# A state-space scan on Trainium2: one scan per block with the carried state as its initial value

## The chip, the cores and the metric

The kernel runs on one core of a Trainium2 chip. The metric is the device time of one execution in microseconds (us). The engines that the text names are TensorE (PE, and PEld for its weight loads), VectorE (DVE), ScalarE (ACT), GpSimd (POOL) and SyncE (SP), which issues most of the DMAs. Each engine has an instruction queue of its own that it works through in order, and the queues are tied together by semaphores.

## The reference, cut to what matters

The layer is a macaron: a feed-forward part with ternary weights (d = 512, 2048 hidden), a Mamba-like mixer, and the feed-forward part again, over 4 sequences of 1024 tokens, each part with a layernorm and a residual. The change touches only the recurrence of the mixer:

```
D, E, N = 512, 1024, 16
def step(h, inp):                       # h: (batch, E, N), zero at a sequence's start
    d_l, B_l, C_l, x_l = inp
    A_bar = jnp.exp(d_l[:, :, None] * A)
    h = h * A_bar + (d_l * x_l)[:, :, None] * B_l[:, None, :]
    y_l = jnp.einsum('ben,bn->be', h, C_l)
    return (h, y_l)
```

Channels are E = 1024 (8 blocks of 128 partitions), and each channel has N = 16 states.

## The kernel before

The 4096 tokens are cut into 16 chunks of CH = 256 tokens (4 chunks a sequence). A chunk's recurrence is worked in STEPS = 32 steps: the first 16 for the channel blocks 0 to 3 ("half 0"), one state n each, the last 16 for the blocks 4 to 7 ("half 1"). So a step S = 32 x chunk + s handles one state of four blocks of 256 tokens, 1024 columns on 128 partitions. Four engines share a step, and a ring of four buffers `h[:, s % RING]` goes round between them:

- POOL, `u_times_b` (L725): `h` = u x B, 1024 columns (L743). Then, since the scan starts from zero at each block's head, it waits for its own product (`ub_step`) and adds the first state's contribution to column 0 of the four blocks (L747, four columns). It releases `ub_ready`. Ahead of the product stand waits for the planes of B (`bb_loaded`), for the ring slot (`hT_ready` or `times_c`) and for `carry_saved`.
- ACT, `exps` (L981): the decays exp(delta x A) for the columns 1 to 255 of each block, in PSUM, two activations for each of two tiles `abar[0]` and `abar[1]` of two blocks. Column 0 of each block stays zero (set once, L1407), so that one scan can run through two blocks and starts afresh at the second one. A tile can be refilled once the scan of the step before has read it.
- DVE, `scan_of` (L1287): two `tensor_tensor_scan`s a step, each over 512 columns (two blocks), with the constant 0.0 as initial value (L1294), in place in `h`.
- ACT, `save_carry` (L993): the last column of each block goes to `carry`. PE, `states_T` (L1515): eight transposes of `h` into PSUM (L1522), and DVE, `y_add` (L1303), adds them into y, scaled by C (L1323, the first of a half L1320). For 8 to 10 steps of a chunk ("elem" steps) POOL multiplies by C instead (`state_times_c`, L757) and adds the product into `xw` by a DMA that accumulates (L761).

The first state of a chunk is made once per half: ACT's `first_decay` (L998) computes exp(delta[0] x A) for 16 states of four blocks (L1003, four activations), DVE's `mask_carry` (L1296) zeroes the carry where a sequence begins, POOL's `first_state` (L763) multiplies both (L768) into `a0`, which L747 adds.

The rest of the layer runs beside this, on the same engines: PE's matmuls of the feed-forward part (L1560, L1571), of the projections (L1583, L1593, L1613, L1632), their evacuation by ACT and DVE, the convolution (DVE L1367, L1376), softplus (ACT, POOL L809), u = delta x x (POOL L850), and POOL's low halves of the hidden values (`hidden_low`, L842). The order is written out by hand: the tables FILL_SLOTS, FIRST_SLOTS, LOOP_SLOTS and LAST_SLOTS say for each of 32 slots of a phase which PE jobs stand in it, and each engine's queue follows from them with fixed offsets (exps 2 slots ahead of the step, the product 3 ahead, the scan 1 ahead, and so on). The phases are fill, first, 14 times loop, last, drain. SP reloads a pair of B's planes (`load_planes`, L647) when POOL's products have used the old one, by `ub_ready`.

Of the kernel before, what the change touches and what calls it, by code (L numbers as in the profile page):

```python
# [21 lines left out]
P = 128  # L22
# [4 lines left out]
CH = 256  # L27
# [196 lines left out]
ACTS = 2  # L224
XD_0 = 3
# [88 lines left out]
def elems_before(c, s):  # L314

    whole = [len(elem_of(k)) for k in range(c)]
    return sum(whole) + sum(k < s for k in elem_of(c))

# [95 lines left out]
def macaron_kernel(nc, resid, norm_w, W_skip, W_in, conv_w, conv_b, W_delta_1, W_delta_2, b_delta_2, W_B, W_C,  # L414
# [12 lines left out]
    with ctx:  # L427
# [40 lines left out]
        a0 = sb("a0", [P, 2, HE, N])  # L468
# [54 lines left out]
        abar_zero = sem("abar_zero")  # L523
# [8 lines left out]
        ub_step, ub_ready, abar_ready = sem("ub_step"), sem("ub_ready"), sem("abar_ready")  # L532
        a0_ready, masked, x0_ready = sem("a0_ready"), sem("masked"), sem("x0_ready")
# [49 lines left out]
        def _(sp):  # L583
# [116 lines left out]
        def _(pool):  # L700
# [24 lines left out]
            def u_times_b(i, s):  # L725
# [3 lines left out]
                if s == 0 or q > planes_of(s - 1):  # L729
                    need(pool, bb_loaded[q % 2], 16 * planes_loaded(i, q))  # L730
                if s % N == 0:
                    if S:
                        u_of(i, half, S)
                    need(pool, u_ready, 2 * i + half + 1)
                    need(pool, x0_ready, 2 * i + half + 1)
# [3 lines left out]
                elif S >= RING:  # L739
# [3 lines left out]
                pl.tensor_tensor(h[:, s % RING, :, :], u[:, :, :],  # L743
                                 bb[:, planes_of(s) % 2, s % PLANES:s % PLANES + 1, :].broadcast_to([P, HE, CH]),
                                 ALU.mult).then_inc(ub_step, 1)
                need(pool, ub_step, S + 1)
                pl.tensor_tensor(h[:, s % RING, :, 0], h[:, s % RING, :, 0], a0[:, half, :, n], ALU.add).then_inc(ub_ready, 1)  # L747

            def state_times_c(i, s):
# [7 lines left out]
                pl.tensor_tensor(hc[:, :, :], h[:, s % RING, :, :], cplane[:, k:k + 1, :].broadcast_to([P, HE, CH]),  # L757
# [87 lines left out]
            def u_of(c, half, S):  # L845
                need(pool, ub_ready, S)
# [19 lines left out]
            def run(ph, i):  # L866
# [3 lines left out]
                for s in range(STEPS):  # L870
# [13 lines left out]
                    for q in range(QT):  # L884
                        if after(ph, f"YT_{q}", 0, s):
                            gated(ph, i, q)
                    for kind, p in hidden_units(ph, s):
                        hidden_low(ph, i, kind, p)
# [4 lines left out]
                    if ph != "fill" and after(ph, "D2_1", 3, s):  # L893
                        first_state(i + 1, 0)
                    if after(ph, "D2_3", 2, s):
                        softplus(i, 1)
                    if after(ph, "D2_3", 3, s):
                        first_state(i, 1)
# [10 lines left out]
        def _(sc):  # L909
# [71 lines left out]
            def exps(i, s):  # L981
# [4 lines left out]
                for r in range(2):  # L986
                    need(sc, scanned, 2 * S - 1 + r)
                    for e in range(2):
                        k = half * HE + 2 * r + e
                        ins = ac.activation(abar[r][:, e, 1:], delta[:, k, 1:], ACT.Exp, scale=a_neg[:, k, n:n + 1])  # L990
                    ins.then_inc(abar_ready, 1)

            def save_carry(i, s):  # L993

                need(sc, scanned, 2 * (STEPS * i + s + 1))
                ac.activation(carry[:, s // N, :, state_of(s)], h[:, s % RING, :, CH - 1], ACT.Copy).then_inc(carry_saved, 1)
# [730 lines left out]
```

## Time and profile before

| | |
|---|---|
| median of 3 runs (lowest to highest) | 2941.11 us (2938.22 to 2942.51) |
| the profiled execution | 2940.29 us, its span 2938.7 us |
| busy over the span | PE 90%, DVE 86%, POOL 82%, ACT 65% |
| mean granted clock of TensorE | 0.97 of full speed |
| one loop iteration (from 1026.40 to 1197.32 us) | 170.92 us |

The profile is one execution. Its page gives busy shares by engine, the chain of work that ended last (followed back from the last instruction to what released it), the costliest groups of instructions and the idle time in front of them. A busy time is a union, so where an instruction starts a little before its predecessor on the same engine has ended, count x mean is more than busy. The trace behind the page answers by stretch, line and engine.

### The profile page before, as it was taken

What the parts mean: (1) busy time and instruction counts of PE and PEld (TensorE: products, weight loads), DVE (VectorE), ACT (ScalarE), POOL (GpSimd) and SP (SyncE); (2) the same over time, 40 slices, a digit from 0 to 9 for tenths busy, and PEclk for the clock granted to TensorE, in tenths of its full rate; (3) what the DMA queues carried; (4) which work ended last, traced back from release to release, by engine and by line L of the source; (5) the groups of instructions that cost most, each with busy time, mean ns of one, the idle gap of its engine ahead of it and who ended that gap; (6) DMA issues with size and microseconds to landing.
All of it is one profiled execution on the core that took longest, in us unless ns stands there. A gap on an engine that the chain in (4) does not pass through costs nothing.

```text
span 2938.7 us, 51656 instructions
## 1 busy us (share of the span) xinstructions
PE 2657.0 (90%) x17527; PEld 2054.0 (70%) x17527; DVE 2534.3 (86%) x3233; ACT 1900.3 (65%) x4428; POOL 2412.7 (82%) x2179
## 2 busy tenths in 40 slices
PE   4776899999999999999999999999999999999778
PEld 4555677776867777686777768677777867777555
DVE  6377899898889999898988989899998989899892
ACT  6375767666676766667676666767666676766651
POOL 1178888888898898989888898998989898897991
PEclk9888899999999999999999999999999999999898
DMA  7022222222222212222222131222213222221320
GB/s 261 31 60 69 62 53 69 49 53 72 51 70 53 70 46 55 73 51 69 53 65 50 48 80 44 71 58 64 51 49 79 48 69 57 65 51 48 87 55 15
DMA packets 91260, 185.22 MB, mean 63 GB/s; under 512 B 12220, under 2 KB 30456, under 8 KB 90488
## 3 DMA queue, kind: packets, MB, share of 16 engines
q1 hardware_dynamic: 72280, 113.76, 12.1%
q0 software_dynamic: 18720, 68.17, 11.8%
q8 instruction: 142, 2.33, 0.3%
q14 instruction: 118, 0.97, 0.1%
HBM read 104.82 MB, written 8.91 MB: 39 GB/s over the span
## 4 chain that ended last, share of the span: by engine, by line
PE 61%; POOL 12%; DVE 8%; ACT 5%; issue 5%; DMA 3%; POOLq 0%; DVEq 0%; ACTq 0%
PE ps L1560 20%; PE ps L1571 14%; PE ps L1583 10%; PE ps L1522 8%; POOL h L743 6%; PE ps L1632 5%; DVE h L1294 4%; DMA xw<-hc 3%; POOL hc L757 2%; PE ps L1593 2%; ACT ps L990 2%; DVE xc L1367 1%; POOL u L850 1%; POOL hl L842 1%; PE ps L1613 1%
## 5 line engine op out<-in xcount | busy, mean ns | idle before, releaser
L743 POOL TENSOR_TENSOR h<-u,bb 128x1024 f32<-128x1024 f32 x512 | 1247.1, 2436 | 82.5 <-PE ps L1522 36.7
L990 ACT ACTIVATE ps<-delta,a_neg 128x255 f32<-128x255 f32 x2048 | 877.0, 470 | 537.8 <-DVE h L1294 536.3
L1294 DVE TENSOR_TENSOR_SCAN h<-ps,h 128x512 f32<-128x512 f32 x1024 | 1189.5, 1203 | 27.3 <-ACT ps L990 13.2
L1560 PE MATMUL ps<-xh,q_up 128*128 128x256 f16 x2048 | 466.7, 275 | 38.0 <-DVE xl L1233 29.7
L1560 PE MATMUL ps<-xh,q_gate 128*128 128x256 f16 x2048 | 466.1, 274 | 28.4 <-DVE xw L1400 28.4
L1323 DVE SCALAR_TENSOR_TENSOR y<-ps,ccur,y 128x512 f32<-128x512 f32 x700 | 487.6, 737 | 1.7 <-PE ps L1522 1.1
L1522 PE MATMUL ps<-ident,h 128*128 128x128 f32 x3056 | 413.7, 278 | 64.0 <-DVE y L1323 58.8
L1560 PE MATMUL ps<-xl,q_up 128*128 128x256 f16 x2048 | 466.6, 275 | 0.0
L1560 PE MATMUL ps<-xl,q_gate 128*128 128x256 f16 x2048 | 465.5, 274 | 0.0
L1522 PEld LDWEIGHTS ps<-ident,h 128*128 128x128 f32 x3056 | 353.8, 142 | 135.4 <-issue 59.0
L842 POOL TENSOR_TENSOR hl<-act,hh 128x512 f16<-128x512 f32 x256 | 314.1, 1231 | 148.7 <-ACT hh L1015 148.7
L1571 PE MATMUL ps<-q_down,hh 128*128 128x512 fp8e4 x1024 | 388.0, 379 | 1.9 <-POOL hl L842 1.0
L1571 PE MATMUL ps<-q_down,hl 128*128 128x512 fp8e4 x1024 | 388.0, 379 | 0.0
L757 POOL TENSOR_TENSOR hc<-h,cplane 128x1024 f32<-128x1024 f32 x130 | 306.9, 2361 | 2.6 <-DMA xw<-hc 2.3
L1583 PE MATMUL ps<-xrT,w_in 128*128 128x256 f32 x1024 | 251.9, 403 | 37.4 <-DVE xc L1367 33.9
L1010 ACT ACTIVATE act<-ps,tanh_sc 128x512 f32<-128x512 f32 x256 | 174.5, 681 | 147.8 <-PE ps L1560 82.2
L1331 DVE SCALAR_TENSOR_TENSOR act<-act,ps 128x512 f32<-128x512 f32 x256 | 173.4, 677 | 108.7 <-ACT act L1010 107.6
L1560 PEld LDWEIGHTS ps<-xh,q_up 128*128 128x128 fp8e4 x2048 | 201.6, 98 | 77.9 <-issue 53.0
L1583 PEld LDWEIGHTS ps<-xrT,w_in 128*128 128x128 f32 x1024 | 201.5, 202 | 70.0 <-DVE xc L1367 37.8
L1560 PEld LDWEIGHTS ps<-xh,q_gate 128*128 128x128 fp8e4 x2048 | 201.6, 98 | 69.5 <-issue 41.5
L1632 PE MATMUL ps<-w_out,gz 128*128 128x512 f32 x512 | 241.8, 606 | 3.8 <-POOL gz L864 3.7
L1583 PE MATMUL ps<-xrT,w_skip 128*128 128x256 f32 x1024 | 231.1, 381 | 0.0
(137 smaller groups left out, 3827.5 us busy)
## 6 DMA issues: line engine op xcount, KB each, us to landing
xw<-hc POOLq DMA_DIRECT2D x130, 512.0 KB, 4.5
bb<-b_scratch SPq DMA_DIRECT2D x224, 256.0 KB, 3.1
cplane<-c_scratch SPq DMA_DIRECT2D x130, 128.0 KB, 3.1
xs<-in_L_attn_resid_dram SPq DMA_DIRECT2D x17, 512.0 KB, 3.7
out_dram<-xs SPq DMA_DIRECT2D x16, 512.0 KB, 4.2
wraw<-in_L_ffn_W_up_dram SPq DMA_DIRECT2D x4, 1024.0 KB, 9.6
wraw<-in_L_ffn_W_gate_dram SPq DMA_DIRECT2D x4, 1024.0 KB, 12.5
wraw<-in_L_ffn_W_down_dram SPq DMA_DIRECT2D x4, 1024.0 KB, 14.1
```

The lines of the kernel that those rows point to most:

```text
L743: pl.tensor_tensor(h[:, s % RING, :, :], u[:, :, :], bb[:, planes_of(s) % 2, s % PLANES:s % PLANES + 1, :].broadcast_to([P, HE, CH]), ALU. ...
L757: pl.tensor_tensor(hc[:, :, :], h[:, s % RING, :, :], cplane[:, k:k + 1, :].broadcast_to([P, HE, CH]), ALU.mult).then_inc(times_c, 1)
L842: pl.tensor_tensor(hl[:, 2 * p:2 * p + 2, :], act[:, p % ACTS, :].rearrange("q (f t) -> q f t", f=2), hh[:, 2 * p:2 * p + 2, :], ALU.subtr ...
L990: ins = ac.activation(abar[r][:, e, 1:], delta[:, k, 1:], ACT.Exp, scale=a_neg[:, k, n:n + 1])
L1010: ac.activation(act[:, p % ACTS, :], pp, ACT.Tanh, scale=tanh_sc[:, 0:1]).then_inc(tanh_ready, 1)
L1294: v.tensor_tensor_scan(hr, abar[r].rearrange("p e t -> p (e t)"), hr, 0.0, ALU.mult, ALU.add).then_inc(scanned, 1)
L1323: ins = v.scalar_tensor_tensor(out=yy, in0=hT[:, t, :], scalar=cc, in1=yy, op0=ALU.mult, op1=ALU.add)
L1522: ins = te.transpose(hT[:, t, e * P:(e + 1) * P], h[:, s % RING, e, t * P:(t + 1) * P], ident[:, :])
L1560: ins = te.matmul(pp[:, f * CH:(f + 1) * CH], w[:, d, col:col + P], part[:, d, :], start=(d == 0 and part is xh), stop=(d == DB - 1 and pa ...
L1571: ins = te.matmul(pp, part[:, f, t * P:(t + 1) * P], q_down[:, f, :], start=(f == 0 and part is hh), stop=(f == FB - 1 and part is hl))
L1583: ins = te.matmul(pp[:, e * CH:(e + 1) * CH], w[:, d, col:col + P], xrT[:, d, :], start=(d == 0), stop=(d == DB - 1))
L1632: ins = te.matmul(pp, gz[:, e, t * P:(t + 1) * P], w_out[:, e, :], start=(e == 0), stop=(e == EB - 1))
```

## The change

Each block gets a scan of its own, 256 columns, and the carried state of that block and state is passed as the scan's initial value, one value per partition. So four scans a step take the place of two. The exps now cover column 0 too, and the zeros in it (L1407), `a0`, `first_decay`, `first_state`, and POOL's small add with the wait on its own product are gone; the first scan of a half waits for `masked` instead. The product releases `ub_ready` itself. The diff also brings lists by which products, gating and low halves could be put on DVE (`UB_ON_DVE`, `Z_ON_DVE`, `LOW_ON_DVE`); all are empty here, so the code that belongs to them issues nothing, and `ub_before(c, s, False)` is 32 c + s. What they leave behind: `bb_loaded` is waited for at each step, `hidden_low` waits for its own previous result, and SP counts one semaphore up once more for each load of planes.

```diff
@@ sync @@
-                    sp.wait_ge(ub_ready, STEPS * (c - (q < 2)) + last + 1)
+                    need(sp, ub_ready, ub_before(c - (q < 2), last + 1, False))
+                    sp.sem_inc(sp_go, 1)
+                    need(sp, dve_ub_ready, ub_before(c - (q < 2), last + 1, True))
                     sp.sem_inc(sp_go, 1)
@@ gpsimd, u_times_b @@
-                if s == 0 or q > planes_of(s - 1):
-                    need(pool, bb_loaded[q % 2], 16 * planes_loaded(i, q))
                 if s % N == 0:
                     if S:
-                        u_of(i, half, S)
+                        u_of(i, half)
                     need(pool, u_ready, 2 * i + half + 1)
-                    need(pool, x0_ready, 2 * i + half + 1)
+                if s in UB_ON_DVE:
+                    return
+                need(pool, bb_loaded[q % 2], 16 * planes_loaded(i, q))
...
-                                 ALU.mult).then_inc(ub_step, 1)
-                need(pool, ub_step, S + 1)
-                pl.tensor_tensor(h[:, s % RING, :, 0], h[:, s % RING, :, 0], a0[:, half, :, n], ALU.add).then_inc(ub_ready, 1)
+                                 ALU.mult).then_inc(ub_ready, 1)
...
-            def first_state(c, half):
-                need(pool, a0_ready, 2 * c + half + 1)
-                need(pool, masked, 2 * c - 1 + half)
-                go()
-                pl.tensor_tensor(a0[:, half, :, :], a0[:, half, :, :], carry[:, half, :, :], ALU.mult).then_inc(x0_ready, 1)
@@ gpsimd, hidden_low @@
                 need(pool, hh_ready, g + 1)
+                need(pool, hl_ready, g)
@@ scalar, exps and first_decay @@
-                        ins = ac.activation(abar[r][:, e, 1:], delta[:, k, 1:], ACT.Exp, scale=a_neg[:, k, n:n + 1])
+                        ins = ac.activation(abar[r][:, e, :], delta[:, k, :], ACT.Exp, scale=a_neg[:, k, n:n + 1])
...
-            def first_decay(c, half):
-                need(sc, delta_ready, 2 * c + half + 1)
-                for e in range(HE):
-                    k = half * HE + e
-                    ins = ac.activation(a0[:, half, e, :], a_neg[:, k, :], ACT.Exp, scale=delta[:, k, 0:1])
-                ins.then_inc(a0_ready, 1)
@@ vector, scan_of @@
-                S = STEPS * i + s
-                need(ve, ub_ready, S + 1)
+                S, half, n = STEPS * i + s, s // N, state_of(s)
+                if s % N == 0:
+                    need(ve, masked, 2 * i - 1 + half)
+                if s in UB_ON_DVE:
+                    need(ve, dve_ub_ready, ub_before(i, s + 1, True))
+                else:
+                    need(ve, ub_ready, ub_before(i, s + 1, False))
                 for r in range(2):
                     need(ve, abar_ready, 2 * S + r + 1)
-                    hr = h[:, s % RING, 2 * r:2 * r + 2, :].rearrange("p e t -> p (e t)")
-                    v.tensor_tensor_scan(hr, abar[r].rearrange("p e t -> p (e t)"), hr, 0.0, ALU.mult, ALU.add).then_inc(scanned, 1)
+                    for e in range(2):
+                        he = h[:, (STEPS * i + s) % RING, 2 * r + e, :]
+                        ins = v.tensor_tensor_scan(he, abar[r][:, e, :], he, carry[:, half, 2 * r + e, n:n + 1], ALU.mult, ALU.add)
+                    ins.then_inc(scanned, 1)
```

## Rows read from the trace of the kernel before

**Rows 1.** The page: busy time by engine, and the chain's shares by engine

```profile
PE 2657.0 (90%) x17527; PEld 2054.0 (70%) x17527; DVE 2534.3 (86%) x3233; ACT 1900.3 (65%) x4428; POOL 2412.7 (82%) x2179
...
PE 61%; POOL 12%; DVE 8%; ACT 5%; issue 5%; DMA 3%; POOLq 0%; DVEq 0%; ACTq 0%
```

**Rows 2.** Busy time by stretch: us, each engine's, PEclk, DMA share, GB/s

```profile
1026.40:1197.32 170.92, 162.62 (x1084) 126.17 (x1084) 155.08 (x199) 115.71 (x276) 150.51 (x136) 0.99 0.24 60
160.00:383.00 223.00, 179.00 (x1123) 138.64 (x1122) 184.26 (x229) 145.95 (x351) 192.38 (x168) 0.90 0.25 61
2615.11:2780.00 164.89, 142.60 (x834) 110.84 (x833) 144.79 (x182) 107.30 (x260) 143.57 (x125) 0.92 0.25 62
```

**Rows 3.** Busy time in the two parts of that iteration

```profile
1026.40:1164.54 138.14, 135.23 (x876) 104.30 (x876) 128.05 (x167) 91.57 (x213) 119.83 (x109) 0.99 0.21 50
1164.54:1197.32 32.78, 27.40 (x208) 21.87 (x208) 27.03 (x33) 24.15 (x64) 30.68 (x28) 1.00 0.37 101
```

**Rows 4.** The chain in the short part: start us, us, what

```profile
1165.86 0.90 ACT a L1003 x4
...
1192.02 5.27 DMA xw<-hc
```

**Rows 5.** The chain from 2699.8 to 2873.5 us, by line

```profile
by line: POOL h L743 29.9%; POOL hc L757 13.6%; issue 12.4%; DMA xw<-hc 10.5%; DVE h L1294 7.2%; PE ps L1571 5.5%; PE ps L1522 4.0%; DVE y L1323 2.8%; POOL hl L842 2.2%; POOL h L747 1.6%; POOL gz L864 1.4%; POOL u L850 1.4%; DVE xw L1400 1.
```

**Rows 6.** VectorE's groups by form: busy us, mean ns, idle before

```profile
L1294 DVE TENSOR_TENSOR_SCAN h<-ps,h 128x512 f32<-128x512 f32 x1024 | 1189.5, 1203 | 27.3 <-ACT ps L990 13.2 <-POOL h L747 7.3
L1323 DVE SCALAR_TENSOR_TENSOR y<-ps,ccur,y 128x512 f32<-128x512 f32 x700 | 487.6, 737 | 1.7 <-PE ps L1522 1.1
...
L1331 DVE SCALAR_TENSOR_TENSOR act<-act,ps 128x512 f32<-128x512 f32 x256 | 173.4, 677 | 108.7 <-ACT act L1010 107.6
...
L1367 DVE SCALAR_TENSOR_TENSOR xc<-ps,vcol,xc 128x253 f32<-128x253 f32 x68 | 29.2, 469 | 17.0 <-ACT hist L1044 17.0
```

**Rows 7.** VectorE's timeline: start us, us (of all merged), what

```profile
1109.86 2.42 DVE L1367 SCALAR_TENSOR_TENSOR xc<-ps,vcol,xc 128x253 f32<-128x253 f32 x6
...
1121.83 1.38 DVE L1323 SCALAR_TENSOR_TENSOR y<-ps,ccur,y 128x512 f32<-128x512 f32 x2
1123.13 2.42 DVE L1367 SCALAR_TENSOR_TENSOR xc<-ps,vcol,xc 128x253 f32<-128x253 f32 x6
...
1215.23 4.56 DVE L1294 TENSOR_TENSOR_SCAN h<-ps,h 128x512 f32<-128x512 f32 x4
```

**Rows 8.** GpSimd's groups by form

```profile
L747 POOL TENSOR_TENSOR h<-h,a 128x4 f32<-128x4 f32 x512 | 106.3, 208 | 40.1
...
L768 POOL TENSOR_TENSOR a<-a,carry 128x64 f32<-128x64 f32 x31 | 19.0, 614 | 0.0
```

**Rows 9.** GpSimd's timeline

```profile
1160.89 2.35 POOL L743 TENSOR_TENSOR h<-u,bb 128x1024 f32<-128x1024 f32 x1
1163.32 0.21 POOL L747 TENSOR_TENSOR h<-h,a 128x4 f32<-128x4 f32 x1
1163.47 2.36 POOL L809 TENSOR_TENSOR delta<-delta,tmp 128x1024 f32<-128x1024 f32 x1
1165.79 2.36 POOL L743 TENSOR_TENSOR h<-u,bb 128x1024 f32<-128x1024 f32 x1
```

**Rows 10.** Waits over the whole span: us, times, longest

```profile
ACT ps L990 <- DVE h L1294: 536.3, 548, 6.1
```

**Rows 11.** SyncE's waits over the whole span

```profile
SPq L652 <- POOL h L747: 2345.4, 222, 28.3
```

**Rows 12.** Scans alone in the same two parts

```profile
1026.40:1164.54 138.14, 59.48 (x52) 0.99 0.21 50
1164.54:1197.32 32.78, 14.86 (x13) 1.00 0.37 101
```

**Rows 13.** Waits of VectorE in the long part, longest and shortest

```profile
DVE xw L1400 <- DMA xw<-hc: 3.1, 2, 1.6
...
DVE xs L1345 <- PE ps L1632: 0.5, 1, 0.5
```

More of the change, by code:

```diff
@@ L224 @@
 ACTS = 2
+UB_ON_DVE = []
+Z_ON_DVE = []
+LOW_ON_DVE = {1: [], 2: []}
 XD_0 = 3
@@ L317, in elems_before, with ub_before @@
     return sum(whole) + sum(k < s for k in elem_of(c))
+def ub_before(c, s, on_dve):
+    mine = [k for k in range(STEPS) if (k in UB_ON_DVE) == on_dve]
+    return len(mine) * c + sum(k < s for k in mine)
 def rows_before(c, s):
@@ L531, in macaron_kernel @@
         bank_used = [sem(f"bank_used{p}") for p in range(NBANK)]
-        ub_step, ub_ready, abar_ready = sem("ub_step"), sem("ub_ready"), sem("abar_ready")
-        a0_ready, masked, x0_ready = sem("a0_ready"), sem("masked"), sem("x0_ready")
+        ub_ready, abar_ready = sem("ub_ready"), sem("abar_ready")
+        dve_ub_ready = sem("dve_ub_ready")
+        masked = sem("masked")
         b_stored, c_stored = sem("b_stored"), sem("c_stored")
@@ L756, in state_times_c @@
                 go()
-                pl.tensor_tensor(hc[:, :, :], h[:, s % RING, :, :], cplane[:, k:k + 1, :].broadcast_to([P, HE, CH]),
+                pl.tensor_tensor(hc[:, :, :], h[:, (STEPS * i + s) % RING, :, :], cplane[:, k:k + 1, :].broadcast_to([P, HE, CH]),
                                  ALU.mult).then_inc(times_c, 1)
@@ L884, in run @@
                     for q in range(QT):
-                        if after(ph, f"YT_{q}", 0, s):
+                        if after(ph, f"YT_{q}", 0, s) and q not in Z_ON_DVE:
                             gated(ph, i, q)
                     for kind, p in hidden_units(ph, s):
-                        hidden_low(ph, i, kind, p)
+                        if p not in LOW_ON_DVE[kind]:
+                            hidden_low(ph, i, kind, p)
                     if after(ph, "DN1_1", 0, s):
@@ L995, in save_carry @@
                 need(sc, scanned, 2 * (STEPS * i + s + 1))
-                ac.activation(carry[:, s // N, :, state_of(s)], h[:, s % RING, :, CH - 1], ACT.Copy).then_inc(carry_saved, 1)
-            def first_decay(c, half):
-                need(sc, delta_ready, 2 * c + half + 1)
-                for e in range(HE):
-                    k = half * HE + e
-                    ins = ac.activation(a0[:, half, e, :], a_neg[:, k, :], ACT.Exp, scale=delta[:, k, 0:1])
-                ins.then_inc(a0_ready, 1)
+                ac.activation(carry[:, s // N, :, state_of(s)], h[:, (STEPS * i + s) % RING, :, CH - 1], ACT.Copy).then_inc(carry_saved, 1)
             def tanh_up(ph, i, kind, p):
@@ L1178, in run @@
                         softplus_log(ph, i, i + 1, 0)
-                    if ph != "fill" and after(ph, "D2_1", 2, s):
-                        first_decay(i + 1, 0)
                     if after(ph, "D2_3", 1, s):
                         softplus_log(ph, i, i, 1)
-                    if after(ph, "D2_3", 2, s):
-                        first_decay(i, 1)
                     for half in range(2):
@@ L1401, in y_plus_x, with hidden_low @@
                 ins.then_inc(bank_used[bk], 1)
+                if q in Z_ON_DVE:
+                    need(ve, bank_used[bk], job_no(ph, i, f"YT_{q}")[1] + 1)
+                    go()
+                    v.tensor_tensor(gz[:, qb, :], yx, gz[:, qb, :], ALU.mult).then_inc(z_ready, 1)
+            def hidden_low(ph, i, kind, p):
+                need(ve, hh_ready, PAIRS * ffn_run(ph, i, kind) + p + 1)
+                need(ve, hl_ready, PAIRS * ffn_run(ph, i, kind) + p)
+                v.tensor_tensor(hl[:, 2 * p:2 * p + 2, :], act[:, p % ACTS, :].rearrange("q (f t) -> q f t", f=2),
+                                hh[:, 2 * p:2 * p + 2, :], ALU.subtract).then_inc(hl_ready, 1)
             def run(ph, i):
@@ L1405, in run @@
                     ve.wait_ge(q_saved, ALL_SAVED)
-                    for r in range(2):
-                        v.memset(abar[r][:, :, 0], 0.0).then_inc(abar_zero, 1)
-                    ve.wait_ge(abar_zero, 2)
                 for s in range(STEPS):
@@ L1412, in run @@
                         scan_of(*step)
+                    for kind, p in hidden_units(ph, s - 1):
+                        if p in LOW_ON_DVE[kind]:
+                            hidden_low(ph, i, kind, p)
                     if s == MASK_H and "IN_0" in PHASES[ph]:
@@ L1429, in run @@
                         ternary(2, 4 + r, r * F, F)
+                    step = step_of(ph, i, s + U_AHEAD)
+                    if step and step[1] in UB_ON_DVE:
+                        u_times_b(*step)
                     for name in results(ph, s, late=True):
```

35 lines of the change are left out of this document (21 added, 14 removed).

## The prediction

> **What bounds the kernel now.** I read the page first, for the shares of the engines and for the chain that ended last [rows 1]: PE is busy 90% of the span and carries 61% of the chain, but VectorE (DVE) is at 86% and GpSimd (POOL) at 82%, so this is no kernel with one bottleneck and idle helpers. The busy time by stretch comes next [rows 2]: one of the 14 equal loop iterations takes 170.92 us and holds 162.62 us of PE, 155.08 of DVE, 150.51 of POOL and 115.71 of ACT. PE has 8.3 us of idle time per iteration, DVE 15.8, POOL 20.4. Then I cut the iteration at the places where the chain changes hands [rows 3]. In a long stretch of 138.14 us PE is busy 135.23, and DVE 128.05: PE sets the pace, DVE has 10.1 us of air. In a short stretch of 32.78 us PE is busy only 27.40 and POOL 30.68: here the chain runs through ACT, POOL's products and the DMA behind them [rows 4]. 5.4 of PE's 8.3 idle us lie here. The end of the kernel is a third regime: from 2699.8 us on, 30% of the chain is POOL L743 and 7% the scans [rows 5].
>
> **The change, part by part.** Two things are removed from POOL, one from ACT, nothing moves to another engine (the new lists are empty), and DVE gets twice as many scans of half the length, each with a per-partition operand in the place of the constant 0.0.
>
> *The scans.* There are 1024 scans of 512 elements, 1.20 us each [rows 6], 64 in an iteration. Back to back they start every 1.12 us: four fill 4.56 us, so (4.56 - 1.20)/3 [rows 7]. That start-to-start time counts, because neighbours on DVE overlap a little. Its fixed part I take from other shapes. Six L1367 (253 elements, one input PSUM, a per-partition scalar) fill 2.42 us, (2.42 - 0.47)/5 = 0.39 each; the pair of L1323 (512 elements, same kinds of operands) starts at 1121.83 and its successor at 1123.13, 0.65 each [rows 7]. So 259 elements cost 0.26 us, 1.0 ns an element, and 0.65 - 0.51 = 0.14 us is fixed, with a scalar operand. Without one (L1331, same shape, constant 1.0) an instruction takes 677 ns where L1323 takes 737 [rows 6], so the operand costs 0.05 to 0.06, and 0.08 is fixed without it. For the scan that gives (1.12 - 0.08)/512 = 2.03 ns an element. A new scan is then 256 x 2.03 ns + 0.08 + 0.05 = 0.65 us, a pair 1.30, against 1.12: **+0.18 us** for each old scan, +11.5 us an iteration, +184 us in all on DVE. Bounds: +0 if a scan's time were all by element (only one size of scan is in this trace, so no row excludes it); +0.08 if the initial operand is read free; +0.35 if neighbours stop overlapping, that is two of 0.65 + 0.08 (1.20 less 1.12). I take 0.18 because L1323 has the scan's kinds of operands in the scan's own neighbourhood.
>
> The Trainium skill (VectorE: DVE Perf Modes, section on the TRN2 errata) speaks against this change too: it puts a fixed 120 cycles on each VectorE instruction with a PSUM source, at 0.96 GHz 125 ns, and advises tiles of at least 512 elements. By that figure alone the extra scans would cost 128 us of DVE time; the trace's fixed part without an operand is smaller, and its operand is extra.
>
> *POOL's small add.* L747 runs 512 times, 208 ns [rows 8]. On the timeline L743 ends at 1163.24, L747 follows, L809 starts at 1163.47; where nothing stands between, L743 starts at 1165.79 right at the end of L809 (1165.83) [rows 9]. So add and wait together are 0.27 us, 8.6 us an iteration, 138 in all. first_state (L768, 31 times, 614 ns [rows 8]) adds 1.2 an iteration. POOL goes from 150.5 to about 140.7. The wait on hl_ready that is added ahead of each hidden_low is for POOL's own last result, finished long before except where two follow each other: at most some 0.05 us for three pairs, nothing. bb_loaded is now waited for at each step instead of each second one; it has been met by then.
>
> *ACT.* first_decay goes, two groups of four activations an iteration, 0.90 us a group, on the chain at 1165.86 [rows 4]. The wait for delta in front of it does not go, it is taken over by the exp that needs delta for the new half. One more element in 2048 exps is below 2 us altogether, hidden in ACT's 536 us of waiting for scans [rows 10].
>
> *Order and queues.* The scan of a half's first step now waits for masked. The mask stands on DVE's own queue, 7 steps (half 0) and 13 steps (half 1) ahead: nothing is late. SP's load of bb is released by L743 instead of L747, 0.3 us sooner; it already waits 2345 us for POOL in total [rows 11], so its two added semaphore increments cost nothing. Ring buffers, carry and the save of the carry keep their order.
>
> **The sum, by stretch.** Long stretch: 52 scans [rows 12] x 0.18 = 9.4 us more on DVE, 128.05 becomes 137.4 in 138.14. Six kinds of waits are named there, 3.1 us down to 0.5, 9.9 in sum [rows 13], for ACT's tanh, for the DMA of hc, for the conv input. They shrink when DVE falls behind, but not to zero, since each has a producer that itself follows DVE; I leave half, 5 us. That makes 142.4, +4.2 us, and PE waits for scans, y adds and banks in it. This is where DVE takes the bound from PE. Short stretch: POOL gives back 5 or 6 adds and a first_state (2.2), ACT 0.9, of which some is spent since DVE gets 12 x 0.18 = 2.2 more in its 5.7 us of air: -1.5. An iteration is then 170.9 + 2.7 = 173.6 us, 14 of them +38. Beginning (160 to 383): some 40 steps, where DVE is at 184 of 223 and POOL at 192 [rows 2]; DVE gets 14 us and POOL gives 11, and I book +1. End, 173.7 us long: 29.9% of it by 2.36 are 22 products of POOL on the chain, x 0.27 = -6; 7.2% by 1.12 are 11 scans, x 0.18 = +2: -4. Sum +35. The profiled execution took 2940.3 us, its span 2938.7, and the median of the runs is 2941.1, so the two agree: **2975 us**.
>
> **The rivals.**
> *DVE saturates and little is hidden (0.25).* The fullest engine now reaches 162.62/170.92 = 0.951 of an iteration. If that is what the coupling of four queues allows, DVE's 155.1 + 11.5 = 166.6 us give 175.2 an iteration, +4.3 x 14 = +60: 3000 us. For it: ACT's exps wait for a scan 548 times [rows 10], and PE's transposes wait behind both. Against it: POOL and ACT get lighter. With a pair price of +0.25, halfway to the upper bound, it is 155.1 + 16 = 171.1, over 0.97 = 176.4: +77, 3017 us. A PE that idles more could also lose clock, which the rows show at 0.99 in the loop and at 0.92 and 0.90 in the ends where PE is less busy [rows 2].
> *POOL's relief wins, faster (0.16).* The place is the short stretch and the end. It decides if the pair costs less than about 0.09 us: then the long stretch gets 52 x 0.09 = 4.7 us into 10.1 of air, keeps its 5 us of real waits and does not grow, while the short one gives 2.5 us in each of 14 iterations and the end 6: -41, 2900 us, and anything up to 2934 with half of it. For it: only the operand-free reading of the initial value is needed. Against it: L1323 with a per-partition scalar is 60 ns dearer than L1331 without [rows 6].
> *Nothing to measure (0.08).* A pair at 0.10 to 0.13 us, where long and short stretch cancel: 2935 to 2947 us.
> *The change not doing what it says.* The instructions are plain to count: 1024 scans more, 512 + 31 adds and 124 activations fewer. What could miss is the claimed relief, if L743 then waits for its ring slot (PE's transposes or hc) instead: POOL's gain would show as idle time. That is inside the forecast, which books only 1.5 us of it.
>
> **How the numbers follow.** Forecast 0.51 (slower, about 2955 to 2990), saturation 0.25 (2990 to 3040), faster 0.16, no change 0.08. Within 0.2%, 5.9 us, is what a measurement of this kernel cannot tell from no change. The range leaves out the best half of the faster case and the last part above a pair price of 0.3 us: 2920 to 3035. The forecast's own range is 2955 to 2990. Faster 0.16, same 0.08, slower 0.76.
>
> **What would show it.** In the profile after: 2048 scans of 256 elements, a single one near 0.73 us, pairs starting 0.65 apart; if they start 0.60 apart, the operand is free. DVE's busy time in an iteration near 166 us, above PE's; DVE's share of the chain up from 8% and PE's down from 61%; ACT's wait for scans longer; POOL's busy time in an iteration near 141 with more idle time ahead of L743, for PE or for DVE. The short stretch should be shorter than 32.8 us and the long one longer than 138. I am wrong if the scans cost what I say and the iteration still stays at 171 us, which would mean that DVE's waits are all slack behind PE; or if DVE's share of an iteration stays well below 0.95 while it grows by over 5 us, which would mean that latency from scan to exp to scan, not occupancy, is what hurts.

## The result, and the profile after

The changed kernel takes 2993.22 us (median of 4 runs, 2983.78 to 3001.29) against 2940.92 us: slower by 1.8%, ratio 1.0178 with a 95% interval of 1.0147 to 1.0209. The profiled execution took 2992.45 us, its span 2990.6, so it is 52.2 us longer than the profiled one before and can be taken apart against it.

The page of the changed kernel, busy time and chain, answers to [rows 1]:

```profile
PE 2677.3 (90%) x17527; PEld 2046.0 (68%) x17527; DVE 2710.1 (91%) x4253; ACT 1885.8 (63%) x4304; POOL 2306.7 (77%) x1636
...
PE 41%; DVE 36%; issue 11%; ACT 6%; POOL 3%; DMA 3%; DVEq 0%; SPq 0%; POOLq 0%; ACTq 0%
```

VectorE has gained 176 us of busy time, POOL has lost 106. VectorE's part of the chain rose from 8% to 36% and PE's fell from 61% to 41%: what ended last is now often a scan.

VectorE by form in the changed kernel (busy us, mean ns, idle before), against [rows 6]:

```profile
L1302 DVE TENSOR_TENSOR_SCAN h<-ps,carry,h 128x256 f32<-128x256 f32 x2048 | 1363.4, 730 | 14.3 <-ACT ps L990 9.6 <-issue 1.3 <-POOL h L753 0.7
L1332 DVE SCALAR_TENSOR_TENSOR y<-ps,ccur,y 128x512 f32<-128x512 f32 x700 | 488.8, 740 | 1.2 <-PE ps L1545 0.6
```

A scan takes 730 ns, and 2048 of them 1363.4 us where 1024 took 1189.5: (1363.4 - 1189.5)/1024 = 0.17 us more for each old scan. On the timeline four now fill 2.67 us, so they start every (2.67 - 0.73)/3 = 0.65 us:

```profile
1165.36 2.67 DVE L1302 TENSOR_TENSOR_SCAN h<-ps,carry,h 128x256 f32<-128x256 f32 x4
```

Busy time by stretch of the changed kernel (columns as in [rows 2]), one loop iteration, the beginning, and the stretch near the end:

```profile
1112.62:1287.60 174.98, 164.20 (x1086) 125.33 (x1085) 166.82 (x264) 114.70 (x266) 143.69 (x102) 0.99 0.24 58
160.00:383.00 223.00, 180.73 (x1122) 138.39 (x1121) 196.49 (x314) 142.76 (x337) 183.28 (x122) 0.90 0.25 61
2752.00:2925.00 173.00, 131.53 (x730) 91.99 (x729) 160.05 (x250) 97.83 (x234) 144.99 (x85) 0.89 0.26 65
```

An iteration lasts 175.0 us with 166.8 of VectorE in it: VectorE has passed PE, and it is busy 95% of the time, just as PE was before [rows 2]. The mean over 13 iterations, from one projection of 32 matmuls on the chain to the one 13 iterations on, is 171.7 us before (405.58 to 2637.96) and 175.2 after (408.16 to 2685.71). So 13 iterations hold 45 of the 52 us, the beginning 2.6, and what follows the last of them 4.2.

Cut at the same events in both (VectorE's add of the half's first y into xw, POOL's add of softplus), the long part of one iteration and the short one, in the kernel before:

```profile
1025.74:1163.47 137.73, 134.17 (x868) 103.50 (x869) 127.64 (x166) 91.16 (x212) 119.42 (x109) 0.99 0.21 51
1163.47:1197.41 33.94, 28.45 (x217) 22.66 (x215) 28.10 (x34) 25.31 (x67) 31.84 (x29) 1.00 0.36 98
```

and in the changed one:

```profile
1044.72:1185.31 140.59, 134.42 (x871) 102.25 (x872) 135.56 (x215) 90.90 (x208) 113.76 (x81) 1.00 0.20 49
1185.31:1219.69 34.38, 29.78 (x215) 23.05 (x213) 31.25 (x48) 24.00 (x61) 30.10 (x22) 0.95 0.36 97
```

The long part grew by 2.9 us, as VectorE went from 127.6 to 135.6. The short part did not shrink. Over all 13 iterations, cut in the same way, the mean long part goes from 138.1 to 140.9 us and the mean short part from 33.6 to 34.2. The granted clock of the short part is 0.95 here, and in five more of the 13, where before it was 1.00 in all but the first; but these six are not longer than the others (33.6 to 34.4 us against 33.6 to 35.9), so no time shows for it.

The chain by line in the short part, before:

```profile
by line: POOL h L743 27.4%; DMA xw<-hc 15.5%; issue 7.1%; POOL hc L757 7.0%; POOL u L850 6.9%; DVE h L1294 5.8%; POOL hl L842 5.0%; ACT ps L990 4.9%; POOL delta L809 3.7%; ACT xh L919 2.9%; ACT a L1003 2.7%; PE ps L1522 2.6%; POOL h L747 2.
```

and after:

```profile
by line: DVE h L1302 15.8%; PE ps L1583 15.3%; DMA xw<-hc 14.9%; PE ps L1655 14.4%; issue 10.1%; POOL h L753 6.9%; POOL hc L765 6.8%; PE ps L1567 3.6%; DVE y L1332 3.3%; PE ps L1545 2.5%; ACT act L1002 2.0%; DVE act L1348 1.9%; DVE xs L1354
```

Most of POOL's products left the chain (27.4% to 6.9%), and scans and PE's matmuls took their place, in nearly the same time. In the 13 short parts before, the chain holds 2.8 small adds each on average, of the 5 or 6 that the prediction counts.

At the end of the kernel the chain by line, against [rows 5], shows the same change of hands, from POOL's products (29.9% to 4.7%) to the scans (7.2% to 33.0%):

```profile
by line: DVE h L1302 33.0%; issue 17.8%; DVE y L1332 9.9%; PE ps L1594 6.4%; POOL h L753 4.7%; PE ps L1545 3.7%; DVE act L1348 2.7%; PE ps L1655 2.5%; DVE act L1340 2.4%; ACT xw L935 1.9%; ACT ps L990 1.8%; DVE xs L1354 1.5%; PE ps L1646 1.
```

Waits over the whole span of the changed kernel (us, times, longest), the first against [rows 10]:

```profile
ACT ps L990 <- DVE h L1302: 708.9, 696, 5.7
POOL hl L844 <- ACT hh L1007: 229.2, 134, 13.2
```

ACT waits 173 us longer for scans, and everything in ACT's queue behind an exp waits with it. POOL, which gave up 106 us of work, waits longer, above all for ACT (148.7 us before).

### The profile page after: what moved, and what is told of

It is laid out like the page before. It is cut to its first block, busy times and chain, and to the rows that moved or that the text cites. A ratio compares the mean times of both kernels' runs of the same rounds, so it can differ in the third digit from the quotient of the medians.

```text
span 2990.6 us, 52708 instructions
## 1 busy us (share of the span) xinstructions
PE 2677.3 (90%) x17527; PEld 2046.0 (68%) x17527; DVE 2710.1 (91%) x4253; ACT 1885.8 (63%) x4304; POOL 2306.7 (77%) x1636
## 4 chain that ended last, share of the span: by engine, by line
PE 41%; DVE 36%; issue 11%; ACT 6%; POOL 3%; DMA 3%; DVEq 0%; SPq 0%; POOLq 0%; ACTq 0%
DVE h L1302 19%; PE ps L1583 16%; PE ps L1606 6%; DVE y L1332 6%; PE ps L1594 5%; PE ps L1545 5%; PE ps L1655 4%; PE ps L1616 3%; DMA xw<-hc 2%; DVE xc L1376 2%; POOL h L753 2%; ACT ps L990 2%; DVE act L1340 2%; DVE xs L1354 1%; POOL hc L765 1%
## 5 line engine op out<-in xcount | busy, mean ns | idle before, releaser
L1302 DVE TENSOR_TENSOR_SCAN h<-ps,carry,h 128x256 f32<-128x256 f32 x2048 | 1363.4, 730 | 14.3 <-ACT ps L990 9.6
L990 ACT ACTIVATE ps<-delta,a_neg 128x256 f32<-128x256 f32 x2048 | 886.9, 470 | 713.4 <-DVE h L1302 708.9
L1545 PE MATMUL ps<-ident,h 128*128 128x128 f32 x3056 | 422.3, 279 | 105.4 <-DVE y L1332 99.7
L1606 PE MATMUL ps<-xrT,w_in 128*128 128x256 f32 x1024 | 239.6, 389 | 28.5 <-DVE xc L1376 24.3
L1606 PEld LDWEIGHTS ps<-xrT,w_in 128*128 128x128 f32 x1024 | 194.4, 195 | 58.5 <-DVE xc L1376 28.2
```

Of the source, the lines that this page charges most:

```text
L990: ins = ac.activation(abar[r][:, e, :], delta[:, k, :], ACT.Exp, scale=a_neg[:, k, n:n + 1])
L1302: ins = v.tensor_tensor_scan(he, abar[r][:, e, :], he, carry[:, half, 2 * r + e, n:n + 1], ALU.mult, ALU.add)
L1545: ins = te.transpose(hT[:, t, e * P:(e + 1) * P], h[:, (STEPS * i + s) % RING, e, t * P:(t + 1) * P], ident[:, :])
L1606: ins = te.matmul(pp[:, e * CH:(e + 1) * CH], w[:, d, col:col + P], xrT[:, d, :], start=(d == 0), stop=(d == DB - 1))
```

## The experiments

Theory A was the prediction's: VectorE's occupancy takes the bound, and POOL's relief gives a part back. Its rivals: latency from scan to exp to scan (B), all of it hidden (C). The first four kernels pull cost and relief apart.

**Cut the scans, keep the constant.** The kernel before with

```diff
-                    v.tensor_tensor_scan(hr, abar[r].rearrange("p e t -> p (e t)"), hr, 0.0, ALU.mult, ALU.add).then_inc(scanned, 1)
+                    for e in range(2):
+                        he = h[:, s % RING, 2 * r + e, :]
+                        ins = v.tensor_tensor_scan(he, abar[r][:, e, :], he, 0.0, ALU.mult, ALU.add)
+                    ins.then_inc(scanned, 1)
```

> The kernel before with each scan of 512 columns cut into two of 256, initial value the constant 0.0 as before; the computation is unchanged, since the zero decay in column 0 already restarts each block. POOL's small add stays. Theory A (VectorE's occupancy takes the bound): a pair starts every 1.20 us instead of 1.12, if the operand alone is what costs the other 0.09 us; VectorE gets about 80 us, 5 us an iteration, and the long part of the iteration grows by 1 to 3 us: 2955 to 2985 us. Theory B (the latency from scan to exp to scan hurts, not occupancy): the same order of growth, as the pair ends 0.08 us later 32 times on the chain of an iteration, 2980 us, with VectorE well below 95% of an iteration. Theory C (VectorE's air hides it): 2941 plus or minus 6.

**Cut the scans, with the carried state.** The same, with `carry[:, s // N, 2 * r + e, n:n + 1]` for `0.0`, n being the step's state, and the wait for `masked` at a half's first step.

> The kernel before with each scan cut in two and with the carried state as the initial value, as in the change; but the zero decay in column 0, first_decay, first_state and POOL's small add stay, so the output is the same. It is the change's cost without its relief. Theory A: slower than the change by what the relief is worth, which the prediction put at 1.5 to 2.5 us in an iteration and 6 at the end: 2993 + 25 to 40 = 3018 to 3033. Rival (POOL's relief is worth nothing, because VectorE now sets the end everywhere): 2993 plus or minus 8.

**The relief alone.** The kernel before with 1024 long scans, and

```diff
-                                 ALU.mult).then_inc(ub_step, 1)
-                need(pool, ub_step, S + 1)
-                pl.tensor_tensor(h[:, s % RING, :, 0], h[:, s % RING, :, 0], a0[:, half, :, n], ALU.add).then_inc(ub_ready, 1)
+                                 ALU.mult).then_inc(ub_ready, 1)
```

and no first_decay and first_state.

> The kernel before with its 1024 scans of 512 columns, but without POOL's small add, first_state and first_decay. It leaves out the carried state, so every chunk starts from zero. It is the change's relief without its cost. Theory A by the prediction's stretches: 2.5 us in each of 14 iterations and 6 at the end, 2900 us. Rival (the relief is behind other engines): 2941 plus or minus 6, POOL's busy time down by 125 us and its idle time up by as much.

**The change without the operand.** The changed kernel with `0.0` for the `carry` operand of the scan.

> The changed kernel with the constant 0.0 in the place of the carried state as initial value; it leaves out the carried state. It shows the price of the per-partition operand in the scan. If the operand costs 0.05 to 0.06 us a scan, as with the scalar operands of the kernel before: scans of about 0.675 us, starting every 0.60 us, VectorE's busy time 2600 us instead of 2710, and about 2993 - 14 x 3.5 + a few = 2950 us. If the operand is free and the fixed part is what costs: 0.73 us and 2993 us.

Measured, against 2939.04 us for the kernel before in the same series:

| kernel | median us | ratio (95% interval) |
|---|---|---|
| scans cut, constant | 2947.35 | 1.0021 (1.0011 to 1.0032) |
| scans cut, carried state | 3003.61 | 1.0214 (1.0197 to 1.0231) |
| relief alone | 2926.44 | 0.9954 (0.9938 to 0.9970) |
| change with constant | 2940.92 | 1.0000 (0.9992 to 1.0009) |

None of the first three met theory A's range. The cut with the constant came out 8 us below theory A's 2955 to 2985 (VectorE gained 41 us, not 80) and at the upper edge of theory C's 2935 to 2947. The cut with the carried state lies below the 3018 to 3033 of A, and 3 us above the rival's band. The relief alone lies between the 2900 of A and the rival's 2935 to 2947. The fourth went as expected, and 9 us further.

Three things follow. First, the price of a scan splits. The scans of the cut kernels by form, constant first, then carried state:

```profile
L1295 DVE TENSOR_TENSOR_SCAN h<-ps,h 128x256 f32<-128x256 f32 x2048 | 1238.0, 666 | 21.9 <-ACT ps L990 12.1 <-POOL h L747 6.1
```

```profile
L1297 DVE TENSOR_TENSOR_SCAN h<-ps,carry,h 128x256 f32<-128x256 f32 x2048 | 1362.4, 727 | 17.1 <-ACT ps L990 9.8 <-POOL h L747 3.0 <-issue 1.4
```

Cutting costs (1238.0 - 1189.5)/1024 = 0.05 us for each old scan, the operand (1362.4 - 1238.0)/2048 = 0.06 us for each new one, 0.12 a pair. Second, the time does not follow in proportion: the cut alone, 41 us more of VectorE on the page (2575.5), cost 8 us; the operand on top, 121 us more, cost 56. The first part of the load falls into VectorE's air, the rest takes the bound. That is the occupancy theory, and it speaks against latency (B), by which each 0.01 us at a pair's end should cost about the same; here 0.05 us a pair cost 8 and 0.12 cost 56. In the constant version VectorE's share of the chain is 17%, in the other one 45%. It is the operand more than the number of scans that makes the change slow: with the constant, relief and cut cancel. Third, the relief is small: 12.6 us alone, 6.4 between the two kernels with the constant and 10.4 between the two with the carried state (2993.22 against 3003.61, from different series). I had expected 25 to 41. Cost and relief add: the scans alone are +64.6, the relief alone -12.6, in sum 52.0, where the whole change measured 52.3.

**Where the relief went.** The trace of the relief alone has the very same VectorE instructions as the kernel before, and 41 us more of VectorE's busy time (2575.2 against 2534.3). Two small masks, which zero the carry and the conv history at a sequence's start, took 50.5 us more; the larger two-input operations took a little less. By form, in the kernel before:

```profile
L1300 DVE TENSOR_TENSOR carry<-carry,keep 128x64 int32<-128x64 int32 x30 | 51.6, 1719 | 0.0
...
L1352 DVE TENSOR_TENSOR hist<-hist,keep 128x24 int32<-128x24 int32 x16 | 2.9, 184 | 0.0
```

and with the relief alone:

```profile
L1289 DVE TENSOR_TENSOR carry<-carry,keep 128x64 int32<-128x64 int32 x30 | 78.2, 2607 | 0.0
...
L1341 DVE TENSOR_TENSOR hist<-hist,keep 128x24 int32<-128x24 int32 x16 | 26.8, 1672 | 0.0
```

The timeline shows what they stand behind. The same mask of the carry in the kernel before, with POOL beside it:

```profile
1147.35 3.28 DVE L1300 TENSOR_TENSOR carry<-carry,keep 128x64 int32<-128x64 int32 x1
```

```profile
1146.78 1.46 POOL L842 TENSOR_TENSOR hl<-act,hh 128x512 f16<-128x512 f32 x1
1147.90 2.64 POOL L743 TENSOR_TENSOR h<-u,bb 128x1024 f32<-128x1024 f32 x1
1150.62 0.21 POOL L747 TENSOR_TENSOR h<-h,a 128x4 f32<-128x4 f32 x1
```

VectorE with the relief alone, then POOL in the same window:

```profile
1138.98 5.25 DVE L1289 TENSOR_TENSOR carry<-carry,keep 128x64 int32<-128x64 int32 x1
1144.16 1.40 DVE L1312 SCALAR_TENSOR_TENSOR y<-ps,ccur,y 128x512 f32<-128x512 f32 x2
```

```profile
1138.08 1.46 POOL L839 TENSOR_TENSOR hl<-act,hh 128x512 f16<-128x512 f32 x1
1139.20 4.94 POOL L742 TENSOR_TENSOR h<-u,bb 128x1024 f32<-128x1024 f32 x2
```

With the relief alone a mask of 64 columns lasts 5.25 us: it begins during a low half and ends when the row of POOL operations without a gap ends (1139.20 + 4.94 = 1144.14). Before, it took 3.28 us and ended with one product (1147.90 + 2.64 = 1150.54), since POOL then waited for its own result ahead of the small add. The Trainium skill (SBUF — State Buffer, section SBUF: two separate sides) has the rule: a VectorE instruction with two SBUF inputs and a GpSimd instruction that reads SBUF share a pair of ports, the one that starts first has it for its whole length, and the other is fully blocked. The trace agrees, and adds that the second can stay out through more than one GpSimd instruction in a row, here the rest of a low half and two products. In the changed kernel the mask stands through the rest of one product and the whole of the next, VectorE first:

```profile
1167.94 4.22 DVE L1309 TENSOR_TENSOR carry<-carry,keep 128x64 int32<-128x64 int32 x1
```

```profile
1167.14 4.94 POOL L753 TENSOR_TENSOR h<-u,bb 128x1024 f32<-128x1024 f32 x2
```

The history's mask is another matter. With the relief alone most of them start 0.4 us into POOL's u = delta x x and last 1.96 us, until it ends; in the kernel before they start 0.05 us before a product's end and last 0.15 us. How long they take is a matter of where they fall.

From this came theory A': taking POOL's small add away also takes away the gaps in which VectorE's two-input operations got in. The rival (D): POOL was never on the path. In 12 of 16 chunks no sequence begins and the mask is all ones, so it can be left out with the same output.

**Masks away, three bases.** To both masks:

```diff
+                if c % CPB:
+                    ve.sem_inc(masked, 1)        # hist_masked in the other
+                    return
```

> The kernel before without VectorE's masks of the carry and of the conv history in the chunks that don't begin a sequence (12 of 16), where the mask is all ones; nothing of the result is left out. The control for the next run. VectorE loses some 40 of 55 us of busy time. Theory A' (VectorE operations with two SBUF inputs stand still while a GpSimd product runs, and the small add's gaps let them in): those masks are short or hidden here, and VectorE isn't the bound, so 2941 less 0 to 8. Theory D (the relief is worth little because POOL was never on the path): the same.

> The kernel with POOL's small add, first_state and first_decay taken away (it leaves out the carried state), and without the masks in 12 of 16 chunks. Theory A': with the small add gone the masks took 105 us of VectorE instead of 55, and that ate part of the relief; without them the relief shows in full, 2926 less 15 to 30, and the difference to the run before (relief with no masks on either side) is 20 to 35 us instead of 13. Theory D: the masks are on nobody's path; the relief stays 13 us.

> The changed kernel without the masks in 12 of 16 chunks. The masks took 79 us of VectorE in it, so about 60 go. Where VectorE sets the pace, three of the runs so far gave 0.4 to 0.6 us of time for each us of its busy time above some 2600: 2993 - 60 x 0.55 = 2960, or somewhat below. If VectorE's occupancy were not the cause of the loss: 2985 to 2995.

**And two more products with C on POOL**: `ELEM = [3, 6, 8, 11, 15, 17, 22, 25, 27, 31]`.

> The same, and in the loop's chunks POOL takes ten of 32 products with C instead of eight. Each takes 1.3 us from VectorE (two y adds) and 0.87 us from PE (eight transposes) and gives POOL 2.36 us and a DMA issue. If VectorE is still the bound of the kernel before this, it gives another 1.3 x 0.5 x 28 = 18 us or more, 2940; if POOL's DMA chain at the half's end gets late instead, it loses: 2960 to 2980.

Measured, against 2940.69 us:

| kernel | median us | ratio (95% interval) |
|---|---|---|
| before, no masks | 2926.82 | 0.9953 (0.9941 to 0.9966) |
| relief alone, no masks | 2885.44 | 0.9811 (0.9796 to 0.9825) |
| change, no masks | 2951.99 | 1.0037 (1.0024 to 1.0049) |
| change, no masks, ten products with C | 2959.08 | 1.0068 (1.0056 to 1.0081) |

Without the masks the relief is worth 2926.8 - 2885.4 = 41 us, with them 13. That has the sign of theory A' and goes beyond its expected 20 to 35, and D falls. The control run also missed its range, by more gain than expected: 14 us, for 37.9 us less of VectorE's busy time (2534.3 to 2496.4). The change's cost over the relief alone is the same on both sides, 66.8 us with masks and 66.6 without.

The traces say where the gain and the cost lie. All are cut at the same events as above, 13 iterations each, in us; a row adds up to the span of that profiled execution:

| kernel | until the first cut | short part, mean | long part, mean | after the last cut |
|---|---|---|---|---|
| before | 304.4 | 33.57 | 138.13 | 402.2 |
| scans cut, carried state | 305.5 | 34.93 | 140.82 | 413.1 |
| change | 306.7 | 34.15 | 140.93 | 407.9 |
| relief alone | 299.8 | 33.36 | 138.10 | 395.0 |
| before, no masks | 303.8 | 33.44 | 137.34 | 401.1 |
| relief alone, no masks | 299.5 | 32.97 | 135.98 | 392.3 |

The scans cost 1.4 us in a short part and 2.7 in a long one. The relief gives back 0.8 in the short part on top of them, and alone 0.2 with masks and 0.5 without. So in the short part the masks hide little of it. What they take is the long part's gain: 1.4 us without them, nothing with them. The rest of the relief lies at the beginning (4 to 5 us) and at the end (7 to 9).

The last run, with ten products, came out at 2959 us, 1 us below the branch that loses (2960 to 2980) and 19 above the one that gains: it lost 7 us, although VectorE fell from 2651.6 to 2617.0. The expected cause is not in the trace: VectorE's wait for POOL's DMAs fell from 14.8 to 10.4 us, and the short part shrank from 33.9 to 33.2. The long part grew from 138.6 to 139.8, and these waits grew with it; with eight products they were 0.8 and 21.4 us:

```profile
PE ps L1600 <- POOL hl L844: 34.5, 15, 2.7
DVE xs L1357 <- PE ps L1600: 65.2, 19, 9.1
```

POOL's low halves came late for PE's matmuls, and VectorE waited for those. That this wait sets the time was not tested.

**A wait in the place of the add.** After each product, in the relief alone and in the changed kernel:

```diff
                                  ALU.mult).then_inc(ub_ready, 1)
+                need(pool, ub_ready, S + 1)
```

> The kernel with POOL's small add, first_state and first_decay taken away (it leaves out the carried state), but after each product POOL waits for its own result, as it did ahead of the small add; no instruction is added. It asks what lets VectorE's two-input masks in. Theory A' (they stand still while GpSimd products follow each other without a gap): the masks fall back from 2607 and 1672 ns to about 1700 and 200 ns, VectorE's busy time from 2575 to about 2535 us, and the time goes from 2926 to 2915 or 2935, as the wait itself costs POOL 0.05 us a step (26 us in all). Rival (the masks' length is a matter of where they happen to fall): masks stay above 2300 and 1200 ns.

> The changed kernel with the same wait of POOL for its own product and nothing else. Theory A': the masks (2133 and 965 ns) get shorter by some 15 to 25 us in all, POOL has air to pay the wait, 2993 less 5 to 15. Rival: 2993 plus or minus 8, or more, masks as long as before.

**One add for two products.**

```diff
+                if s % 2 == 0:
+                    return
                 need(pool, ub_step, S + 1)
-                pl.tensor_tensor(h[:, s % RING, :, 0], h[:, s % RING, :, 0], a0[:, half, :, n], ALU.add).then_inc(ub_ready, 1)
+                two = h[:, s % RING - 1:s % RING + 1, :, 0]
+                pl.tensor_tensor(two, two, a0[:, half, :, n - 1:n + 1].rearrange("p e n -> p n e"), ALU.add).then_inc(ub_ready, 2)
```

> The kernel before with one small add for two products: columns 0 of two ring slots in one instruction, released after the second product. 512 scans of two blocks stay, so VectorE pays nothing, and POOL has 256 small adds fewer (about 0.25 us each, 64 us, 4 an iteration). The first product of a pair is released a slot later. With the masks in place the contention takes its part: 2941 less 3 to 12. If the later release hurts (VectorE waits for POOL's product): 2945 to 2960.

> The same without the masks in 12 of 16 chunks. The whole relief was worth 41 us on this base (2926.8 to 2885.4); half of the adds gone should give about half, 2906. If the later release hurts: 2925 or more.

Measured, against 2941.59 us:

| kernel | median us | ratio (95% interval) |
|---|---|---|
| relief alone, own wait | 2913.31 | 0.9902 (0.9888 to 0.9917) |
| change, own wait | 2980.81 | 1.0135 (1.0116 to 1.0154) |
| one add for two products | 3117.38 | 1.0593 (1.0575 to 1.0610) |
| the same, no masks | 3098.73 | 1.0524 (1.0506 to 1.0542) |

An added wait, and nothing else, made both kernels faster by 12 to 13 us (against their medians in the earlier series, whose base lay within 3 us of this one's; for the changed kernel the intervals of the two ratios just touch). The masks of the relief alone with the wait, by form:

```profile
L1290 DVE TENSOR_TENSOR carry<-carry,keep 128x64 int32<-128x64 int32 x30 | 49.8, 1661 | 0.0
L1342 DVE TENSOR_TENSOR hist<-hist,keep 128x24 int32<-128x24 int32 x16 | 3.6, 227 | 0.0
```

They are back at the lengths of the kernel before. For the carry's mask the timeline shows the gap at work, VectorE first:

```profile
1136.40 3.20 DVE L1290 TENSOR_TENSOR carry<-carry,keep 128x64 int32<-128x64 int32 x1
```

```profile
1136.86 2.65 POOL L742 TENSOR_TENSOR h<-u,bb 128x1024 f32<-128x1024 f32 x1
1139.71 2.37 POOL L742 TENSOR_TENSOR h<-u,bb 128x1024 f32<-128x1024 f32 x1 [0.20 <-POOL h L742]
```

It begins under a low half as before and ends with one product, not two: 3.20 us, not 5.25. So it is the gap that lets it in, and not the add. For the history's mask the rival holds. With the wait it starts 0.1 us ahead of u instead of 0.4 into it, and with the scans cut and the carried state, where POOL's small add is in place, it took 1591 ns. No run had the wait and no masks, so how much of the 13 us comes by the masks is not shown. The masks of the changed kernel, without the wait and with it:

```profile
L1309 DVE TENSOR_TENSOR carry<-carry,keep 128x64 int32<-128x64 int32 x30 | 64.0, 2133 | 0.0
L1361 DVE TENSOR_TENSOR hist<-hist,keep 128x24 int32<-128x24 int32 x16 | 15.4, 965 | 0.0
```

```profile
L1310 DVE TENSOR_TENSOR carry<-carry,keep 128x64 int32<-128x64 int32 x30 | 35.9, 1198 | 0.0
L1362 DVE TENSOR_TENSOR hist<-hist,keep 128x24 int32<-128x24 int32 x16 | 19.6, 1222 | 0.0
```

The carry's mask fell from 2133 to 1198 ns, the history's rose from 965 to 1222: 24 us less in sum, as expected, but not each by itself.

One add for two products was the clear miss, far above the 2945 to 2960 expected for a release that hurts; without masks it lies 174 us above the 2925 that was given as the least. The waits of that kernel name it:

```profile
ACT ps L993 <- DVE h L1297: 719.2, 656, 5.7
DVE h L1297 <- POOL h L750: 251.9, 128, 5.5
```

Scans waited 252 us for POOL's products, against 7.3 before [rows 6]. The product stands two slots ahead of its scan, but the first of a pair was now released after the second, and POOL's queue in between holds waits for ring slots and for ACT: its products waited 186.2 us for PE's transposes, which free the slots, against 36.7 before. The lead was on paper in slots; in microseconds it was not there.

The kernel before without the 24 masks of the carry and 12 of the history that do nothing is the fastest with the full computation, 2926.8 us, 0.5% better than before and 2.2% better than the change.

## Why the prediction was right, and where its terms were not

The direction was right by its mechanism: a scan's price was forecast well, and VectorE took the bound from PE in the long part. That the sum came so close is in part luck, since two terms were wrong in opposite directions. Over 13 iterations the long part came out 18 us cheaper than booked and the short part 27 us dearer; the beginning added 1 and the end 7, which makes the 17 us by which the profiled execution lies above the sum.

- **Direction and size.** 2993 lies inside 2920 to 3035, slower as forecast. It lies 18 us above the point, beyond the forecast's own 2955 to 2990 by 3, and inside the saturation rival (2990 to 3040). That rival's iteration of 175.2 us was met: VectorE now fills 166.8/175.0 = 0.953 of an iteration, where PE filled 0.951. The forecast's 173.6 us was too short by 1.6.
- **The scan's price.** Forecast +0.18 us, measured 0.17. The split was a little off: 0.05 for the cut and 0.12 for two operands, against 0.08 and 0.10. The method, start-to-start times and neighbours with the same kinds of operands, held. The 125 ns that the prediction cites from the Trainium skill (VectorE: DVE Perf Modes, section on the TRN2 errata) agree with single durations, 2 x 666 - 1203 = 129 ns, but an extra scan among neighbours cost 47.
- **The long part.** Forecast +4.2 us, measured +2.8 in the mean: in the iteration shown VectorE kept 5.0 us of idle time, the 5 us that were booked, but only 7.9 us of work came on top, not 9.4. The part holds 51 old scans before and 100 new ones after, so one pair less, which is 1.3 us.
- **The short part and the end** are where the sum failed. I booked -1.5 us an iteration; the mean was +0.6. After the 13th iteration I had booked one more iteration and the end, 2.7 - 4 = -1.3 us; measured was +4.2 to +5.7, by where one cuts. The failing step is "POOL gives back 5 or 6 adds and a first_state (2.2), ACT 0.9". Of these 3.1 us, 0.8 came. The scans took 1.4 of it back, near the 1.6 that I had allowed. POOL did shed the work, as listed, but only 2.8 of the adds stood on the chain, and when POOL's products left it, scans and PE's matmuls made up nearly the same time. That this is the whole of the missing 2.3 us is not shown. I had put the whole relief of POOL on the path, and no other chain beside it.
- **The masks.** A second term was missing. I had costed the small add by POOL alone and did not ask who used the pause behind each product. In the changed kernel the masks cost VectorE 25 us more than before (79.4 against 54.5), 0.8 us in each short part. The mask's 1719 ns for 64 columns stood in the trace of before, against 184 ns for its smaller sister, and I passed over it.
- **POOL's busy time.** I took 0.27 us an add off it, and got 140.7 us an iteration; 143.7 were measured. The add was busy 0.21 us, the rest was wait. That the reading was wrong did not touch the sum.
- **The faster rival** put 41 us on a full relief. Alone, with masks, it was 13; without them, 41, but that agreement is luck: its terms were 2.5 us in each short part and 6 at the end, and the table above shows 0.5 there, 1.4 in the long part, and the rest at both ends. Its deciding price of 0.09 us a pair was wrong too: at 0.05 (the constant) it forecast 2900 us, and 2940.9 were measured. Its "2934 with half of it" should read 2920, half of 41 below 2941.
- **Order and queues.** That the waits on masked, on bb_loaded and SP's increments cost nothing agrees with VectorE's 14.3 us of idle time before all 2048 scans; no run took these waits out by themselves.

## What to carry to other kernels

Before an instruction is cut into shorter ones with a per-partition operand, find the fixed part and the operand's part in start-to-start times of neighbours on the same engine, and put their sum against the idle time of that engine in the stretch where it is fullest: here the first 41 us on VectorE cost 8, and of the next 121 about half was paid. And look at what an engine's small pauses are good for before you remove them: in these traces a short VectorE operation with two SBUF inputs waited for whole GpSimd instructions, and with no pause between these for several. A short operation whose mean time is several times its shortest (1719 ns against 200 here) is the sign of it, in the kernel before any change. Last, before work is taken off an engine, count what of it stands on the chain, and look at which chain runs beside it: here a quarter of the relief booked for the short part came.

## What the runs showed of the hardware that was not expected

- A VectorE operation of 64 columns and two SBUF inputs took 0.20 us when it began with POOL between instructions and 5.25 us when it began under a low half and two POOL products followed without a gap: it did not get in between them. Operations with one input in PSUM (the y adds, 737 ns with the relief as without) did not notice.
- Adding a wait of POOL for its own result after each product shortened the whole kernel by 13 us (2926.4 to 2913.3) and brought that mask from 5.25 to 3.20 us, one POOL product instead of two.
- An initial value per partition costs a scan 0.06 us (727 ns against 666). The y adds, with a scalar operand, take as much more than an operation of the same shape without one (737 ns against 677), although the scan has twice their time per column.
